# Two moved loops and a stored transpose in a four-stage Trainium2 kernel (search for tokens, turned tokens, output projection)

## What is computed

```python
x = x + LN(attn0(LN(x)))   # causal attention, 16 heads of 16, rotated q and k
x = x + LN(mod(LN(x)))     # router picks 128 of 1024 tokens of a batch (top_k of x @ w_router);
                           # these pass through attention and a gated MLP and go back to their places
x = x + LN(sparse(LN(x)))  # per head the 35 queries with the largest max-minus-mean over 35 sampled
                           # keys attend to all 1024 keys; every other row is the mean of v; then Wo, bo
x = x + LN(ffn(LN(x)))     # LN, 256 -> 1024 silu -> 256, weights given as integers and scales
```

## Time and profile before

| | us |
|---|---|
| median of 3 runs (lowest, highest) | 2852.1 (2850.38, 2854.42) |
| the profiled execution's own time | 2849.34 |
| its span | 2847.4 |
| busy in the span: PE, DVE, ACT, POOL | 2528.7, 1724.6, 1196.6, 895.6 |
| attention, token stage, sparse stage (by the first instructions) | 0 to 1452, to 1851, to 2847 |

### The profile page before, as it was taken

How to read it: one execution, slowest core, us unless ns; L and a number is a source line. 1 busy time by engine, 2 the same in 40 slices (tenths; PEclk the granted TensorE clock), 3 DMA queues, 4 the chain that set the end, 5 groups by cost and what they waited for, 6 DMA issues and landing times. The chain is left out here.

```text
span 2847.4 us, 40820 instructions
## 1 busy us (share of the span) xinstructions
PE 2528.7 (89%) x14324; PEld 1501.4 (53%) x14324; DVE 1724.6 (61%) x4778; ACT 1196.6 (42%) x1949; POOL 895.6 (31%) x1420
## 2 busy tenths in 40 slices
PE   5999999999999999899628999966999999999997
PEld 2444444444444444344317888744566665666664
DVE  7767685767767676787758665626544344454442
ACT  1556566656656665656412342122232223222321
POOL 4130614416061441603231221114323315224142
PEclk8899999999999999999858999978999999999999
DMA  5252441615244061522120122221002101011010
GB/s 176 54 157 54 134 121 37 184 41 181 71 130 124 33 199 34 164 84 64 46 87 24 43 70 64 83 75 61 31 32 74 46 30 61 31 60 46 16 45 30
DMA packets 156156, 220.27 MB, mean 77 GB/s; under 512 B 18629, under 2 KB 123025, under 8 KB 149714
## 3 DMA queue, kind: packets, MB, share of 16 engines
q1 hardware_dynamic: 151858, 213.65, 24.5%
q0 software_dynamic: 4096, 4.01, 0.5%
HBM read 113.75 MB, written 103.88 MB: 76 GB/s over the span
## 5 line engine op out<-in xcount | busy, mean ns | idle before, releaser
L1106 ACT ACTIVATE pt<-ps 128x1024 f32<-128x1024 f32 (+3 forms) x768 | 600.2, 811 | 337.6 <-PE ps L1002 243.7
L890 DVE CUSTOM_DVE_ANT_0 masked<-ps,mask_q 128x128 bf16<-128x128 f32 (+3 forms) x1024 | 472.8, 484 | 186.7 <-PE ps L978 184.4
L978 PE MATMUL ps<-sk,sq 96*128 96x512 bf16 (+3 forms) x1536 | 430.7, 338 | 66.3 <-DVE mx L890 21.5
L999 PE MATMUL ps<-sq,sk 99*128 99x512 bf16 (+3 forms) x1536 | 398.9, 329 | 10.0 <-DMA sq<-scratch_nm_parts 8.2
L894 DVE TENSOR_REDUCE mx<-ps 128x1 f32<-128x512 f32 x512 | 351.2, 686 | 90.6 <-PE ps L978 90.0
L978 PEld LDWEIGHTS ps<-sk,sq 96*128 96x128 bf16 x1536 | 132.2, 97 | 391.0 <-DVE mx L890 106.2
L1018 PE MATMUL ps<-pt,val 128*32 128x512 f32 (+3 forms) x3072 | 328.6, 500 | 2.4 <-ACT yt L1114 2.4
L2321 PE MATMUL ps<-w_fc,eyb 128*128 128x256 f32 x1024 | 228.0, 380 | 8.2 <-ACT eyb L2382 8.2
L999 PEld LDWEIGHTS ps<-sq,sk 99*128 99x128 bf16 x1536 | 147.7, 98 | 155.0 <-ACT pt L1106 53.6
L2309 PE MATMUL ps<-eht,w_fc 128*128 128x512 f32 x512 | 223.1, 594 | 1.9 <-ACT eht L2372 1.9
L2321 PEld LDWEIGHTS ps<-w_fc,eyb 128*128 128x128 f32 x1024 | 191.9, 190 | 41.1 <-ACT eyb L2382 16.5
(11 more groups left out here) (342 smaller groups left out, 4369.5 us busy)
## 6 DMA issues: line engine op xcount, KB each, us to landing
scratch_stacks<-space SPq DMA_DIRECT2D x32, 768.0 KB, 4.4
sq<-scratch_stacks SPq DMA_DIRECT2D x32, 768.0 KB, 8.6
sk<-scratch_stacks SPq DMA_DIRECT2D x32, 768.0 KB, 9.6
scratch_stacks<-space SPq DMA_DIRECT2D x32, 512.0 KB, 5.0
scratch_x<-xr SPq DMA_DIRECT2D x16, 1024.0 KB, 7.8
space<-in_L_attn_x SPq DMA_DIRECT2D x8, 1024.0 KB, 14.2
scratch_stacks<-space SPq DMA_DIRECT2D x32, 256.0 KB, 5.9
xr<-in_L_attn_x SPq DMA_DIRECT2D x8, 1024.0 KB, 6.3
```

The lines of the kernel that those rows point to most:

```text
L890: nc.vector.tensor_tensor_reduce(mem["masked"][:, slot, 0:n], ps[:, RING[slot], 0:n], mem["mask_q"][:, BANK - n:BANK], 1.0, -3e38, ALU.add ...
L978: nc.tensor.matmul(ps[:, bank, 0:n], sq[0:ROWS, h, i * P:(i + 1) * P], sk[0:ROWS, h, half * BANK:half * BANK + n], start=True, stop=True)\
L999: last = nc.tensor.matmul(ps[:, bank, 0:n], sk[0:ROWS_M, h, j * P:(j + 1) * P], sq[0:ROWS_M, h, q0:q0 + n], start=True, stop=not diag)
L1106: nc.scalar.activation(pt[:, u % 3, 2 * pair:2 * pair + 2, 0:n], ps[:, bank:bank + 2, 0:n], ACT.Exp, scale=SCALE).then_inc(e["exp_done"], 1)
```

## The change

It has four parts. In `attention_steps` the search has 8 rounds ahead of the last set where it had 6, laid in one instruction to a group in the groups 10 to 27 of the turn of batch 6 and 10 to 15 of that of batch 7; the last set has 8 rounds where it had 10; and `tok` stands in group 6 after the last turn, where it stood at its end. For batches 0 to 6, `proj` of tile i-1 stands ahead of `t2` of tile i in the list of a group, where it stood behind it. In the token stage SP also stores the turned tokens (`scratch_xnt`, 1 MB a batch), and ACT waits for the store before it writes `xnt` again. The sparse stage loads them from there into two buffers, has no `xt`, and sums them on DVE in `xm`. In `prob_order`, `cxt` and `wo` stand ahead of the first half of `f2`.

```diff
-TOP_LIGHT = 6
+TOP_LIGHT = 8
...
             put(behind + 9 + i, ("t2", b, i))
-            if i:
+            if b < B - 1:
+                put(behind + 10 + i, ("proj", b, i))
+            elif i:
                 put(behind + 9 + i, ("proj", b, i - 1))
-        put(behind + 17, ("proj", b, NT - 1))
+        if b == B - 1:
+            put(behind + 9 + NT, ("proj", b, NT - 1))
...
-    light = [now + n_eu * s + g for s in range(-SETS, SETS - 1) for g in (9, 10, 11)]
+    beside_products = [now - turn + g for g in range(10, 28)] + [now + g for g in range(10, 16)]
...
-    put(now + 48, ("tok", B - 1))
+    put(now + turn + 6, ("tok", B - 1))
...
                 elif kind == "store_q":
+                    until_taken(sp, "xt", b, 0)
+                    until_taken(sp, "xt", b, 1)
+                    sp.dma_start(io["xnt"][b].rearrange("p (k t) -> p k t", k=KC), xnt[:, :, :]).then_inc(e["xnt_stored"], 16)
...
                     if b:
                         until_filled(act, "q", b - 1, n)
+                        act.wait_ge(e["xnt_stored"], 16 * b)
                     nc.scalar.copy(xnt[:, :, n * BANK:(n + 1) * BANK], src).then_inc(taken, 1)
...
-            order += of(b, "xt", range(NHALF), range(KC))
-            order += [("load_xn", b + 1)] if b + 1 < B else []
+            order += [("load_xnt", b + 1)] if b + 1 < B else []
...
+        if attention:
+            order += of(b, "cxt", range(NHALF), range(KC)) + of(b, "wo", tiles)
         if forward:
             order += of(f, "f2", range(4))
-        if attention:
-            order += of(b, "cxt", range(NHALF), range(KC)) + of(b, "wo", tiles)
...
-                elif kind == "load_xn":
-                    sp.wait_ge(e["xnt_full"], NHALF * KC * b)
-                    sp.dma_start(xn[:, :, :], tokens("xn2", b)).then_inc(e["xn_in"], 16)
+                elif kind == "load_xnt":
+                    if b >= 2:
+                        sp.wait_ge(e["xm_ready"], b - 1)
+                        sp.wait_ge(e["v_full"], NT * (b - 1))
+                    sp.dma_start(xnt[:, b % 2, :, :], io["xnt"][b].rearrange("p (k t) -> p k t", k=KC))\
+                        .then_inc(e["xnt_in"][b % 2], 16)
...
-                    v.wait_ge(e["xnt_ready"], NHALF * KC * (b + 1))
-                    nc.vector.tensor_tensor(xmean[:, :], xsum[:, :, 0], xsum[:, :, 1], ALU.add)
+                    v.wait_ge(e["xnt_in"][b % 2], 16 * (b // 2 + 1))
+                    nc.vector.tensor_reduce(xmean[:, :], xnt[:, b % 2, :, :], AX.X, ALU.add)
...
-                if kind == "xt":
-                    n, k = a
-                    pe.wait_ge(e["xn_in"], 16 * (b + 1))
-                    if b and n:
-                        pe.wait_ge(e["att_ready"], NT * b - 1 + k)
-                    turned(xn, 2 * n + k, n, k, "xnt_full")
...
-                    pe.wait_ge(e["xnt_ready"], NHALF * KC * (b + 1))
+                    pe.wait_ge(e["xnt_in"][b % 2], 16 * (b // 2 + 1))
...
                     pe.wait_ge(e["xm_ready"], b + 1)
+                    if b:
+                        pe.wait_ge(e["att_ready"], NT * b)
```

More of the change, by code:

```diff
@@ L1901, in prob_loop @@
         mem = {
-            "xn": m.sb("exn", [P, NT, C]), "at": m.sb("eat", [MR, B, MT], U32),
+            "at": m.sb("eat", [MR, B, MT], U32),
             "qg": m.sb("eqg", [MR, MT, D]), "qx": m.sb("eqx", [MR, MT, C]), "own": m.sb("eown", [MR, MT, H]),
-            "xnt": m.sb("exnt", [P, KC, T]), "kt": m.sb("ekt", [P, KC, T]), "vv": m.sb("evv", [P, NT, C]),
-            "xsum": m.sb("exsum", [P, KC, NHALF]), "xmean": m.sb("exmean", [P, KC]),
+            "xnt": m.sb("exnt", [P, 2, KC, T]), "kt": m.sb("ekt", [P, KC, T]), "vv": m.sb("evv", [P, NT, C]),
+            "xmean": m.sb("exmean", [P, KC]),
             "qbd": m.sb("qbd", [P, KC, HU]), "obd": m.sb("obd", [P, KC, HU]),
@@ L1928, in prob_loop @@
         e["ctx_in"] = [m.sem(f"e_ctx_in{n}") for n in range(NHALF)]
+        e["xnt_in"] = [m.sem(f"e_xnt_in{n}") for n in range(2)]
         prob_all(nc, io, w, ps, mem, e)
@@ L1935, in prob_all @@
     order = prob_order()
-    (xn, at, qg, qx, own, xnt, kt, vv, xsum, xmean, xmr, vmb, qbd, obd, nmx, nb, sums, pr, pt, red, rows, cx, cxt, astats,
-     amv, xstats, xmv, rstats, rmv, att, x, hh, ht, yb) = (mem[n] for n in """xn at qg qx own xnt kt vv xsum xmean xmr vmb
+    (at, qg, qx, own, xnt, kt, vv, xmean, xmr, vmb, qbd, obd, nmx, nb, sums, pr, pt, red, rows, cx, cxt, astats,
+     amv, xstats, xmv, rstats, rmv, att, x, hh, ht, yb) = (mem[n] for n in """at qg qx own xnt kt vv xmean xmr vmb
         qbd obd nmx nb sums pr pt red rows cx cxt astats amv xstats xmv rstats rmv att x hh ht yb""".split())
@@ L1952, in _ @@
                 sp.dma_start(at[:, 0, :], io["top_rows"][0].rearrange("(m r) -> r m", r=MR)).then_inc(e["first_at_in"], 16)
-                sp.dma_start(xn[:, :, :], tokens("xn2", 0)).then_inc(e["xn_in"], 16)
+                sp.dma_start(xnt[:, 0, :, :], io["xnt"][0].rearrange("p (k t) -> p k t", k=KC)).then_inc(e["xnt_in"][0], 16)
                 sp.dma_start(at[:, 1:GB, :], io["top_rows"][1:GB].rearrange("b (m r) -> r b m", r=MR))\
@@ L2215, in _ @@
                         last = nc.tensor.matmul(ps[:, u % 2, :], w["ps_wk"][:, k, cc * P:(cc + 1) * P],
-                                                xnt[:, k, n * BANK:(n + 1) * BANK], start=(k == 0), stop=(k == KC - 1))
+                                                xnt[:, b % 2, k, n * BANK:(n + 1) * BANK],
+                                                start=(k == 0), stop=(k == KC - 1))
                     last.then_inc(e["kt_full"], 1)
@@ L2230, in _ @@
                     for k in range(KC):
-                        last = nc.tensor.matmul(ps[:, 4 + j % 2, 0:C], xnt[:, k, j * P:(j + 1) * P],
+                        last = nc.tensor.matmul(ps[:, 4 + j % 2, 0:C], xnt[:, b % 2, k, j * P:(j + 1) * P],
                                                 w["ps_wv"][:, k, :], start=(k == 0), stop=(k == KC - 1))
@@ L2328, in _ @@
                 kind, b, a = step[0], step[1], step[2:]
-                if kind == "xt":
-                    n, k = a
-                    act.wait_ge(e["xnt_full"], NHALF * KC * b + KC * n + k + 1)
-                    if b:
-                        act.wait_ge(e["xm_ready"], b)
-                    nc.scalar.activation(xnt[:, k, n * BANK:(n + 1) * BANK], ps[:, 2 * n + k, :], ACT.Identity,
-                                         accum_out=xsum[:, k, n:n + 1]).then_inc(e["xnt_ready"], 1)
-                elif kind == "qx":
+                if kind == "qx":
                     for k in range(KC):
@@ L2388, in build_program @@
     io["top_rows"] = nc.dram_tensor("scratch_top_rows", (B, HU), U32, kind="Internal").ap()
+    io["xnt"] = nc.dram_tensor("scratch_xnt", (B, P, KC * T), F32, kind="Internal").ap()
     io["ctx"] = nc.dram_tensor("scratch_ctx", (B, T, C), F32, kind="Internal").ap()
```

9 lines of the change are left out of this document (5 added, 4 removed).

## The result

The changed kernel takes 2810.3 us (median of 4, 2809.61 to 2811.11) where the kernel before takes 2852.9 (2850.38 to 2854.42) in the same series: ratio 0.9859, 95% interval 0.9847 to 0.9872. The profiled execution has a span of 2807.8 us, 39.6 less.

What follows compares the result with a forecast made beforehand. PE was taken to bound sparse turns and nearly the attention turns, DVE the search's end and b = 1's entry. Terms summed to 27.8 us off 2849.3, 2821.5; with 2.8 for the median, 2824; range just below 2813 to 2839.

Steps and rivals of the forecast that it cites:

- Part 1: End of the search: two rounds fewer in the last set and `t1` straight behind the cast save 9.2 us.
- Part 2: Attention turn 6: 18 search instructions beside the products instead of 12, at 0.6 us each, cost 1.6 us.
- Part 3: Attention turns: projection ahead of the turn back, mostly off the path, saves 0.3 us in each of seven turns, 2 us.
- R3: Rival, attention turns: PE waits for the order of projection and turn back; 12.8 us saved instead of 2, 2813; chance 0.12.
- Part 4: Token stage: the eight 1 MB stores of turned tokens are covered by the time between ACT's copies; 0 us.
- Part 5: Entry of the sparse stage, b = 0: it waits for the gather of queries, so removed transposes give 0 us.
- Part 6: Sparse turns: without `xt` and the wait of `kt`, 2.51 us saved at each of six boundaries, 15.1 us.
- Part 7: Sparse turns: `cxt` and `wo` ahead of the first half of `f2` take away PE's wait for `eyb`; 5.2 us saved.
- R4: Rival, sparse turns: the context lands too late for `cxt`, so the kernel is slower, 2866 if 6 us late; chance 0.03.
- Part 8: Entry of b = 1: DVE is the bound and nothing hides the new sum of 2.2 us; costs 2.1 us.
- R1: Rival, attention turn 6: added search instructions cost DVE their full 1.33 us each, 13 us less saved, 2837; chance 0.08.
- R2: Rival, sparse turns: `kt` waits for something else as long as `xt` took, 15 us lost, 2839; chance 0.03.

Runs made afterwards that it cites:

- e11: Changed kernel with the token step `tok` put back in front of `t1`, at the end of the last set; 2814.7 us, ratio 0.9863.
- e1: Kernel before with only the projection ahead of the turn back, batches 0 to 6; 2839.4 us, ratio 0.9964.
- e6: Changed kernel with DVE alone taking each projection one maximum later, PE's order unchanged; 2838.5 us, ratio 0.9975.
- e3: Kernel before with only the turned tokens: stored, loaded in the sparse stage, no `xt`, sum in `xm`; 2832.8 us, ratio 0.9944.
- e2: Kernel before with only the search moved (8 light rounds, 8 in the last set) and `tok` behind `t1`; 2839.5 us, ratio 0.9969.
- e4: Kernel before with only `cxt` and `wo` ahead of the first half of `f2`; 2843.3 us, ratio 0.9982.
- e7: Changed kernel with the sum of the second batch's tokens taken while the first context is on its way, not in `xm`; 2807.0 us, ratio 0.9867.
- e5: The changed kernel once more, with no edit; 2811.2 us, ratio 0.9884 to the kernel before.
- e9: Changed kernel with DVE's first statistics of each projected tile taken one maximum later, the projection itself unmoved; 2807.7 us, ratio 0.9851.
- e10: Changed kernel with all of the second batch's `xm` (sum and mean row) taken while the first context is on its way; 2807.8 us, ratio 0.9841.

## Why the prediction was right or wrong

- **Part 1, end of the search (+9.2):** right. The last turn lost 9.7 us against before, 9.2 to 9.7 against the three old ones, and `tok`'s share is 1.5 (e11).
- **Part 2, search beside the products (-1.6):** about -1, within the scatter of a turn. The sum was near, but one of its grounds was not: that turn 6 took 9.3 us more than turn 5 was one execution; the same code takes 177.5 and 178.3 in others, where the profile I had shows 175.8.
- **Part 3, projection ahead of the turn back (+2):** this is the step that failed. It was 10.7. I bounded it with 12.8, had it as the rival R3 with 2813 us and gave it 0.12, and I took 0.3 a turn because "PE's own idle time in that stretch is 3.65 us for all causes". Two things were wrong. I took a small share of that idle time without a row that gave the share, and called the place "mostly off the path"; in e1 1.0 us of idle time went in the two stretches behind the first projection, and 0.8 more that had counted as busy, so that idle time was not all there was to win. And the question to ask was which bank the projection takes and when DVE gives it back: the pair of rows (turn back, projection) with 0.45 us between starts, where e1 needs 0.22, stood in the trace of before, and the weight loads of the projection waited 0.28 and 0.37 us for DVE's maxima. R3's size was right. Of its ground, DVE's 1.3 us at every projection, e6 shows that taking the wait away does not help if the bank comes back later (27 us lost); e1 takes 2.2 us of it away in a turn and gains 1.7. How much of the 1.7 is the bank and how much the earlier maxima stays open.
- **Part 4, the store (0):** right. The token stage takes 283.0 us in the mean of the four profiled kernels without the store and 282.9 in the ten with it.
- **Part 5, entry b = 0 (0):** 17.1 us to the first `eqx` in the mean without, 16.5 with; +0.6. If the load of the second batch holds the gather up, then by under 1 us: POOL waits 5.22 us for it, where it was 5.47, and the last gather lands 6.0 to 6.1 us behind its issue with the new load issued 1.1 and 1.6 us ahead of it (changed kernel, e3), 5.1 to 6.2 without (e1, e2, e4). The Trainium skill, "DMA: Bandwidth & Descriptors", section "Queues, rings and completion order", has engines change rings only between packets. The 3.5 us that I had worked out for that case show in no run.
- **Part 6, no `xt` (+15.1):** 16.5. The idle time of 0.76 us in the row counts from a modelled end; from start to start `kt` came 0.92 us closer to `eqx` (1.50 to 0.58).
- **Part 7, context ahead of `f2` (+5.2):** 0.90 a turn in e4, 6.3 in all if turn 1 has it too, which e4 alone does not show. The wait for the context (R4) stayed away from turn 1 on, but for one turn of this profile. In the turn shown its two halves landed at 2338.36 and 2339.92, 3.9 and 5.0 us behind their issues, and PE's weight load for the first stood at 2340.20. In the next turn they took 5.8 and 6.8 us, the weight loads waited 0.35 and 0.28 us for them, and `cxt` took 0.1 us longer. So the margin was of the size that I had put, and it is used up when a load is 2 us late.
- **Part 8, entry b = 1 (-2.1):** right at the place. Between the last statistics and the base row there are now 2.75 us instead of 0.63, the sum takes 2.25 (I took 2.2), and e7 wins it back. The row of the scaling (1.23) would have misled. The Trainium skill, "VectorE: DVE Perf Modes", section "The perf-mode tier table (the rule you actually need)", gives a reduction the 1x rate alone. The 2.25 us agree with that. PE starts base and `v` at a mean granted clock of 0.65 over 4.3 us; that is no new cost, since it was 0.61 before. In e5 it was 0.50 there, and the distance from `eqx` to the first scores 1.0 us longer than in the changed kernel with the same code.
- **The sum** (9.4 and the 0.2 of `tok` as worked out, the rest as measured): 9.4 - 1.0 + 10.7 + 0 + 0.6 + 16.5 + 6.3 - 2.1 - 0.2 (`tok` behind `t1`) = 40.2, against 27.8. Of the 12.4 between them 8.7 are part 3. R1 and R2 did not occur: the new search costs about 1 us more than the old one, and no `kt` waits for its tokens.

Open: what besides the three late projections makes up the 1.7 us of a turn, why the earlier release in e9 shifts 0.3 us from the second stretch of a turn to the first, and the 6 us by which the token stage differs between executions of the same code.

## What to carry to other kernels

- Where engines share a ring of PSUM banks, follow for each step which earlier use its bank had and when that was given back. Here the long step in front of the short one gave DVE time, and the short one in front of the long one made PE pause. The order of two independent steps was worth 1.7 us a turn, and giving one bank back a maximum later cost 4.9 (turns 1 to 5 of e6 against e5).
- Idle time of PE in windows and brackets is not all that can be won in a dense stretch (0.8 of 1.8 us lay in busy time here): compare start to start with the same pair elsewhere, and read the brackets of the weight loads.
- When a wait is taken away in an order written by hand, look at the next in-order step of the engine that gives the results: in e10 the wait only moved from one bank to the next.

## What the runs showed that I had not expected

- PE counted the same 187 products as 0.78 us more "busy" in 27.6 us; its rows showed no wait at the two late projections, its weight loads 0.28 and 0.37 us.
- Each projection read a maximum later on DVE, with nothing else changed, cost 27 us in 2811: 6.5 us of waits of PE in the turn that was read.
- Turn 6 of the attention stage, with the same code, took 175.8, 177.5 and 178.3 us in three kernels, while the steady sparse turns agree within 0.02 us (114.34 to 114.36).
